# Maxima of the attention pairs half a pair further ahead, two PSUM banks for them and four for the scores, and 97-row weights loaded as 96 + 1 rows

## The reference, cut to what matters

```
qkv = win @ qkv_w.T + qkv_b                      # 192 inputs and a bias row: 97 rows for the second half
attn = einsum('bnd,bmd->bnm', q * scale, k)      # + rel_h + rel_w, both made from q
attn = softmax(attn, axis=-1)                    # 196 positions of a window
out = (attn @ v) @ proj_w.T + proj_b
```

## Time and profile before

| what | value |
|---|---|
| median of 3 runs (lowest, highest) | 718.72 us (714.18, 724.86) |
| the profiled execution's own time | 724.53 us |
| its span, first to last instruction | 722.6 us |
| busy: TensorE, VectorE, ScalarE, POOL | 85%, 41%, 30%, 19% |
| mean granted TensorE clock | 0.864 |
| images turned and projected | from 14 to 81 us |
| position terms, maxima of pair 0 | 81 to 125.5 us |
| pairs 0 to 5 start at | 125.5, 153.9, 181.1, 205.1, 233.9, 261.3 us |
| granted clock rises to 1.00 in pairs 0 to 4 at about | 139.7, 170.4, 190.9, 221.6, 249.0 us (steps 3 to 5) |
| and falls to 0.50 at about | 153.4, 187.5, 204.6, 235.3, 262.6 us |
| last product of pair 5 ends | 290.9 us |
| DMA moved | 53.6 MB |

### The profile page before, as it was taken

One profiled execution on the slowest core, in us unless ns is written; L12 is line 12 of the kernel. 1 busy time (PEld: TensorE's weight loads), 2 busy tenths in 40 slices (PEclk: granted clock), 3 DMA queues, 4 the chain that ended last, 5 costly groups with the idle time before them and its releaser, 6 DMA issues.

```text
span 722.6 us, 13520 instructions
## 1 busy us (share of the span) xinstructions
PE 612.8 (85%) x4592; PEld 498.3 (69%) x4593; DVE 294.5 (41%) x899; ACT 220.4 (30%) x554; POOL 137.1 (19%) x113
## 2 busy tenths in 40 slices
PE   0599989979978979899999998995079999999991
PEld 0477886746655755855558896785069999999991
DVE  4353444635735521711123363454613333333331
ACT  1013322334333333132232323132024444444440
POOL 7020100610000000000000031404403333333332
PEclk9999955677968675799999997986579999999997
DMA  2722575937527440490000000104313233233321
GB/s 84 168 66 63 178 185 110 189 102 106 76 37 101 71 78 9 138 414 40 1 1 0 1 29 17 44 1 137 89 29 45 44 44 42 43 43 44 44 37 17
DMA packets 32969, 53.63 MB, mean 74 GB/s; under 512 B 6458, under 2 KB 26484, under 8 KB 31410
## 3 DMA queue, kind: packets, MB, share of 16 engines
q1 hardware_dynamic: 24962, 43.51, 25.3%
q0 software_dynamic: 7968, 9.60, 7.8%
HBM read 32.95 MB, written 20.29 MB: 74 GB/s over the span
## 4 chain that ended last, share of the span: by engine, by line
PE 60%; issue 5%; DVE 5%; SPq 4%; DMA 4%; ACT 2%; POOL 2%; DVEq 0%; POOLq 0%
PE ps L1634 10%; PE ps L1620 7%; PE ps L1327 5%; PE ps L1625 5%; PE ps L1465 4%; PE ps L1453 3%; PE ps L1364 3%; PE ps L1318 3%; PE ps L1522 2%; PE ps L1607 2%; POOL xs_d L553 2%; DMA qa<-erow 2%; PE ps L1457 2%; PE ps L1535 1%; PE ps L1553 1%
## 5 line engine op out<-in xcount | busy, mean ns | idle before, releaser
L566 POOL DMA_INDIRECT out<-ys,place_i x39 | 69.2, 1776 | 123.1 <-DMA out<-ys,place_i 101.6
L1634 PE MATMUL ps<-w2e,hts 128*128 x468 | 82.7, 327 | 1.5 <-DVE ys L1164 1.5
L1634 PEld LDWEIGHTS ps<-w2e,hts 128*128 128x128 f32 x468 | 75.1, 190 | 1.9 <-issue 1.8
L872 DVE TENSOR_REDUCE negm<-ps 98x2 f32<-98x392 f32 x96 | 49.1, 554 | 50.8 <-PE ps L1282 50.4
L553 POOL DMA_INDIRECT xs_d<-rows,slot_i x32 | 31.6, 987 | 192.6 <-DVE slot_i L1076 184.1
L742 ACT ACTIVATE hts<-ps,wst 128x128 f32<-128x128 f32 x234 | 64.5, 383 | 2.2 <-PE ps L1625 2.2
L1327 PE MATMUL ps<-qa,ka 48*98 48x196 f32 x384 | 57.4, 431 | 8.4 <-ACT pt L635 6.1
L635 ACT ACTIVATE pt<-ps 98x392 f32<-98x392 f32 x96 | 42.5, 494 | 61.4 <-PE ps L1327 61.4
L1620 PE MATMUL ps<-xst,wst 128*128 128x128 f32 x468 | 60.0, 279 | 1.1 <-ACT xst L575 1.1
L1620 PEld LDWEIGHTS ps<-xst,wst 128*128 128x128 f32 x468 | 58.4, 195 | 1.7 <-issue 1.7
L575 ACT ACTIVATE xst<-ps 128x256 f32<-128x256 f32 x39 | 15.0, 384 | 121.8 <-PE ps L1607 121.8
(11 more groups left out here) (212 smaller groups left out, 1006.0 us busy)
## 6 DMA issues: line engine op xcount, KB each, us to landing
w1e<-in_w1e SPq DMA_DIRECT2D x8, 579.0 KB, 11.2
w2e<-in_w2e SPq DMA_DIRECT2D x8, 576.0 KB, 12.0
xs<-xs_d SPq DMA_DIRECT2D x39, 98.0 KB, 2.0
ka<-k_d SPq DMA_DIRECT2D x12, 170.0 KB
k_d<-kst SPq DMA_DIRECT2D x16, 121.5 KB, 1.9
x<-in_xp SPq DMA_DIRECT2D x4, 384.0 KB, 19.2
q_d<-qt SPq DMA_DIRECT2D x2, 768.0 KB, 5.5
qa<-q_d SPq DMA_DIRECT2D x12, 128.0 KB
```

The lines of the kernel that those rows point to most:

```text
L566: nc.gpsimd.indirect_dma_start(acc, bass.IndirectOffsetOnAxis(ap=place_i[:, j % 2:j % 2 + 1], axis=0), ys[:, j % 2, :], None, compute_op=A ...
L872: nc.vector.tensor_reduce(dst, src, X, ALU.max, negate=True).then_inc(s["m_red"], 1)
L1634: last = mm(ps[:, 5, 0:D], hts[:, u, k, :], w2e[:, ds(e, 1), k, :], start=(k == 0), stop=(k == HT - 1))
```

## The change

- `wqkv`, `wproj` and `wb`, which have 97 rows, are each loaded by two DMAs, of 96 rows and of 1; semaphore counts follow.
- The maxima of a pair are made in two halves. In pair p, steps 0 to 4 hold units 10 to 19 of p+1, two a step, step 5 none, and steps 6 to 9 units 0 to 9 of p+2 (2, 3, 3, 2). The turn of p+1 is at step 6. Units 0 to 9 of pair 1 stand before pair 0, behind `relative(3)`.
- Product 4 of the pair before and the waits for values, f32 loads and maxima rows stand between units 10 and 11 and the scores of step 0.
- Banks: maxima 0 and 1, the turned maxima in 1; scores 2, 3, 4, 7. A maxima unit waits for the reduction two units back; a score step for the exponentials of two steps back.
- SyncE in pair p: stores of p-1, f32 loads of p+1, maxima rows of p+1, then, when the maxima matmuls of p+1 are done, the bf16 loads of p+3. Those of pair 2 stand before the loop, behind a wait for the stores of the position terms. VectorE's and SyncE's loops over pairs are written out.

The core of the diff (the waits for 13 in place of 11 loads are left out on VectorE and TensorE):

```diff
@@ -55,12 +55,14 @@
-MAX_AT = [range(a, b) for a, b in ((0, 2), (2, 4), (4, 6), (6, 9), (9, 13), (13, 17), (17, 20))] + [range(0)] * 3
-MAX_BANKS = (0, 1, 7)
-SCORE_BANKS = (2, 3, 4)
+MAX_AHEAD = 10
+MAX_AT = [range(a, b) for a, b in ((10, 12), (12, 14), (14, 16), (16, 18), (18, 20), (20, 20),
+                                   (0, 2), (2, 5), (5, 8), (8, 10))]
+MAX_BANKS = (0, 1)
+SCORE_BANKS = (2, 3, 4, 7)
 LINKS = 31
 INVERT_AT = 2
-TURN_AT = 7
+TURN_AT = 6
@@ -290,7 +292,8 @@
             sp.dma_start(ident[:], a["ident"]).then_inc(s["ident_in"], 16)
-            sp.dma_start(wqkv[:], a["wqkv"]).then_inc(s["w1_in"], 16)
+            sp.dma_start(wqkv[0:C], a["wqkv"][0:C]).then_inc(s["w1_in"], 16)
+            sp.dma_start(wqkv[C:C + 1], a["wqkv"][C:C + 1]).then_inc(s["w1_in"], 16)
             for j in range(1, 4):
@@ -383,37 +386,39 @@
             load_pair(1, 1, 0)
-            def pair_step(p, n, more, rows=True):
-                if more:
-                    sp.wait_ge(s["m_ps"], 20 * p + 20)
-                    load_pair(p + 2, n, 1)
-                if rows:
-                    max_rows(p + 1, 1 - n)
+            for k in range(2):
+                sp.wait_ge(s[f"rel_out{k}"], 64)
+            load_pair(2, 0, 1)
+            def store_outputs(p, to_dram):
                 sp.wait_ge(s["o_ok"], 1 + 2 * p + 2)
...
                         src = ot[r:r + HD, :, :].rearrange("p k t -> p (k t)").rearrange("p (bp t) -> p bp t", bp=4)
-                        if more:
-                            dst = o_d[ds(HD * e + 2 * HD * p, HD), :]
+                        if to_dram:
+                            dst = o_d[HD * e + 2 * HD * p:HD * e + 2 * HD * p + HD, :]
                         else:
...
                         sp.dma_start(dst[:, :, TOK * par:TOK * par + TOK], src).then_inc(s["o_out"], 16)
-                if more:
-                    load_pair(p + 2, n, 0)
-            with sp.Fori(0, NPAIR // 2 - 1) as it:
-                for n in range(2):
-                    pair_step(2 * it + n, n, True)
+            for p in range(NPAIR - 1):
+                n = p % 2
+                if p > 0:
+                    store_outputs(p - 1, True)
+                    load_pair(p + 1, 1 - n, 0)
+                max_rows(p + 1, 1 - n)
+                if p + 3 < NPAIR:
+                    sp.wait_ge(s["m_ps"], 20 * (p + 1) + 20)
+                    load_pair(p + 3, 1 - n, 1)
...
             sp.dma_start(ao[0:2 * HD, 1, :], o_d[C:C + 2 * HD, :]).then_inc(s["ao_in"], 16)
-            pair_step(NPAIR - 2, 0, False)
+            store_outputs(NPAIR - 2, False)
@@ -523,15 +528,17 @@
-            for dst, name in ((wproj, "wproj"), (win, "win"), (wout, "wout"), (wb, "wb"), (dft, "dft"), (idft, "idft"),
-                              (ab1, "ab1")):
+            for dst, name in ((wproj, "wproj"), (wb, "wb")):
+                nc.gpsimd.dma_start(dst[0:C], a[name][0:C]).then_inc(s["w2_in"], 16)
+                nc.gpsimd.dma_start(dst[C:C + 1], a[name][C:C + 1]).then_inc(s["w2_in"], 16)
+            for dst, name in ((win, "win"), (wout, "wout"), (dft, "dft"), (idft, "idft"), (ab1, "ab1")):
                 nc.gpsimd.dma_start(dst[:], a[name]).then_inc(s["w2_in"], 16)
...
-            pool.wait_ge(s["w2_in"], 16 * 11)
+            pool.wait_ge(s["w2_in"], 16 * 13)
             late_op(nc.gpsimd.tensor_scalar(aw1[:, :, 2, :], aw1[:, :, 1, :], -1.0, None, ALU.mult))
@@ -629,15 +636,15 @@
                     if tu < 4:
-                        dst, src = pte[:, tu % 2, tu // 2, :], ps[:, SCORE_BANKS[tu % 3], 0:NIMG * EDGE]
+                        dst, src = pte[:, tu % 2, tu // 2, :], ps[:, SCORE_BANKS[tu % 4], 0:NIMG * EDGE]
                     else:
-                        dst, src = pt[:, (tu - 4) % 8, :], ps[0:98, SCORE_BANKS[tu % 3], 0:2 * WIN]
+                        dst, src = pt[:, (tu - 4) % 8, :], ps[0:98, SCORE_BANKS[tu % 4], 0:2 * WIN]
                     nc.scalar.activation(dst, src, ACT.Exp).then_inc(s["t_exp"], 1)
...
                 act.wait_ge(s["m_turned"], p + 1)
-                nc.scalar.activation(mrow[:, n, :], ps[0:16, MAX_BANKS[2], 0:WIN], ACT.Copy).then_inc(s["m_row_ok"], 1)
-                nc.scalar.activation(erow[:, n, :], ps[0:8, MAX_BANKS[2], 2 * P:3 * P], ACT.Copy).then_inc(s["m_row_ok"], 1)
+                nc.scalar.activation(mrow[:, n, :], ps[0:16, MAX_BANKS[1], 0:WIN], ACT.Copy).then_inc(s["m_row_ok"], 1)
+                nc.scalar.activation(erow[:, n, :], ps[0:8, MAX_BANKS[1], 2 * P:3 * P], ACT.Copy).then_inc(s["m_row_ok"], 1)
@@ -864,11 +871,11 @@
                     dst = negm[0:98, n, 8 * e + b:8 * e + b + 17:16]
-                    src = ps[0:98, MAX_BANKS[mu % 3], 0:2 * WIN].rearrange("p (q k) -> p q k", q=2)
+                    src = ps[0:98, MAX_BANKS[mu % 2], 0:2 * WIN].rearrange("p (q k) -> p q k", q=2)
                 else:
...
                     dst = nege[:, n, 4 * e + 2 * hb:4 * e + 2 * hb + 2]
-                    src = ps[:, MAX_BANKS[mu % 3], :].rearrange("p (q k) -> p q k", q=2)
+                    src = ps[:, MAX_BANKS[mu % 2], :].rearrange("p (q k) -> p q k", q=2)
                 nc.vector.tensor_reduce(dst, src, X, ALU.max, negate=True).then_inc(s["m_red"], 1)
@@ -894,26 +901,31 @@
-            def pair(p, n, first, last):
-                for mu in range(20):
-                    if INVERT_AT <= mu < INVERT_AT + 4 and not first:
-                        sums_out(p - 1, 1, mu - INVERT_AT)
-                    if not last:
+            def pair(p, n):
+                first = p == 0
+                for mu in range(MAX_AHEAD, 20):
+                    step = mu - MAX_AHEAD - INVERT_AT
+                    if 0 <= step < 4 and not first:
+                        sums_out(p - 1, 1, step)
+                    if p + 1 < NPAIR:
                         maxima(p + 1, 1 - n, mu)
-                for step in range(4):
-                    sums_out(p, 0, step)
+                for mu in range(MAX_AHEAD):
+                    if p + 2 < NPAIR:
+                        maxima(p + 2, n, mu)
+                    step = mu - MAX_AHEAD + 4
+                    if step >= 0:
+                        sums_out(p, 0, step)
...
             relative(3)
-            pair(0, 0, True, False)
-            with dve.Fori(0, NPAIR // 2 - 1) as it:
-                pair(2 * it + 1, 1, False, False)
-                pair(2 * it + 2, 0, False, False)
-            pair(NPAIR - 1, 1, False, True)
+            for mu in range(MAX_AHEAD):
+                maxima(1, 1, mu)
+            for p in range(NPAIR):
+                pair(p, p % 2)
             for step in range(4):
@@ -1222,7 +1234,7 @@
             turn_image(0, 0, first=True)
-            pe.wait_ge(s["w1_in"], 16)
+            pe.wait_ge(s["w1_in"], 32)
             with pe.Fori(0, NIMG // 2 - 1) as it:
@@ -1269,11 +1281,11 @@
             def max_unit(p, n, mu):
-                bank = MAX_BANKS[mu % 3]
-                if mu == 2:
+                bank = MAX_BANKS[mu % 2]
+                if mu == 1:
                     pe.wait_ge(s["m_row_ok"], 2 * p)
-                if mu >= 3:
-                    pe.wait_ge(s["m_red"], 20 * p + mu - 2)
+                if mu >= 2:
+                    pe.wait_ge(s["m_red"], 20 * p + mu - 1)
                 else:
@@ -1299,14 +1311,14 @@
                 for q in range(2):
-                    nc.tensor.transpose(ps[0:16, MAX_BANKS[2], 98 * q:98 * q + 98], negm[0:98, n, 16 * q:16 * q + 16],
+                    nc.tensor.transpose(ps[0:16, MAX_BANKS[1], 98 * q:98 * q + 98], negm[0:98, n, 16 * q:16 * q + 16],
                                         ident[0:98, 0:98])
-                nc.tensor.transpose(ps[0:8, MAX_BANKS[2], 2 * P:3 * P], nege[:, n, :], ident[:]).then_inc(s["m_turned"], 1)
+                nc.tensor.transpose(ps[0:8, MAX_BANKS[1], 2 * P:3 * P], nege[:, n, :], ident[:]).then_inc(s["m_turned"], 1)
...
-                pe.wait_ge(s["t_exp"], 1 + 20 * p + (2 * j - 1 if j else 0))
-                banks = [SCORE_BANKS[(2 * j + e) % 3] for e in range(2)]
+                pe.wait_ge(s["t_exp"], 1 + 20 * p + max(2 * j - 2, 0))
+                banks = [SCORE_BANKS[(2 * j + e) % 4] for e in range(2)]
                 if j == 0:
@@ -1365,31 +1377,31 @@
-            def pair(p, n, itp, first=False, last=False):
-                more = not last
-                pe.wait_ge(s[f"lf{n}"], itp * 128 + 128)
-                pe.wait_ge(s["m_in"], 64 * p + 64)
-                pe.wait_ge(s["v_pair"], 2 * p + 2)
-                if more:
-                    pe.wait_ge(s[f"lb{1 - n}"], (itp + n) * 128 + 128)
+            def pair(p, n):
+                first = p == 0
                 for j in range(10):
-                    if first and j == 1:
-                        rel_done(pe, 3)
-                    if more and j == TURN_AT:
+                    if j == TURN_AT and p + 1 < NPAIR:
                         max_turn(p + 1, 1 - n)
-                    mus = list(MAX_AT[j]) if more else []
```

(26 more changed lines are left out.)

## The result

The changed kernel takes **696.57 us** (median of 4 runs, 692.51 to 698.00) against 721.79 us (714.18 to 733.64, 4 runs) for the kernel before: a ratio of **0.9676 [0.9573, 0.9778]**, 3.2% faster. Ratios leave out executions more than 1.5% above the fastest of their kernel; medians and ranges hold all of them. The forecast was 693, with a range from 673 to 709. The profiled execution took 698.0 us (span 696.1), 26.5 less than the one profiled before; its mean granted clock is 0.874, against 0.864.

A forecast was written before the change was run, and what follows sets the result against it. TensorE was taken as the bound, losing time to the wqkv load, border and exponential waits and a low clock. Terms summed to -25.5 us: 699 for the profiled execution, 693 against the median, range 673 to 709.

The forecast's parts named there:

- wqkv: At the start, loading it as 96 + 1 rows uses all DMA engines and ends TensorE's wait: -10.9 us.
- Prologue: Ahead of pair 0, ten maxima units of pair 1 delay the first scores: +7.2 us, bounds +5.2 and +8.
- Borders: Between pairs, all 14.4 us of TensorE's waits for maxima rows go; late landing of those rows gives back +2.
- Four score banks: In score steps, the 8.4 us of waits for exponentials go; bounds -6 and -8.4.
- Two maxima banks: In pairs 0 to 4, maxima units stall on VectorE's reductions: +10 us, bounds +2 and +15.
- The clock: Pairs 1, 3 and 4 run low for 8 us each, 24 us less at half speed: -12; pair 5 stays low.
- The rule by which this term would be 0: Skill's psum-queue depth-cycling: brief, frequent idles while cycling PSUM banks swing TensorE's clock; sum would end 12 us higher.
- D: At the start, the split does nothing, because x tiles and not wqkv hold it: 704 us; chance 0.05.
- E: In all pairs, two banks tie TensorE to VectorE and thinner maxima never lift the clock: 739 us; chance 0.03.
- B: In the pairs, the clock isn't regained and the -12 becomes 0: 705 us; chance 0.22.
- C: At four borders, waits return as f32 loads and rows land, 2 us each: 705 us at worst; chance 0.12.
- A: Pair 5 keeps the high clock too, 13 us less: 680 us; chance 0.20.

The follow-up runs named there:

- f1: The kernel before with one edit, wqkv loaded as 96 + 1 rows; 709.94 us.
- g3: The changed kernel with three maxima banks for the thirty units ahead of pair 0 only; 691.31 us, ratio 0.9470 to the kernel before.
- f4: The changed kernel without the ten maxima units ahead of pair 0, whose own steps hold all twenty of pair 1; 698.58 us.
- i4: The changed kernel with the bf16 loads of pair p+3 ahead of the maxima rows of p+1 on SyncE; 701.45 us, ratio 0.9668 to the kernel before.
- i1: The changed kernel with three score banks and still two for maxima, bank 7 idle; 714.46 us, ratio 0.9793 to the kernel before.
- g1: The changed kernel itself, unedited, timed again; 696.06 us, ratio 0.9619 to the kernel before.
- g2: The changed kernel with three maxima and three score banks as before the change, timed in more rounds; 685.98 us, ratio 0.9463 to the kernel before.
- f2: The kernel before with wqkv split and two maxima, four score banks, in the old order of steps; 716.61 us, ratio 0.9955.
- old banks: The changed kernel with three banks for maxima and three for scores; 688.25 us, and 685.98 us when run again.

## Why the prediction was right, and where it was off

**wqkv: right, -12.4 for -10.9.** The mechanism is as forecast, and f1 gives -13.6. The 1.5 us more in the profile are matmuls: the work between turning image 1 and turning image 2 takes 7.9 us and not 9.3, because more of it has the shorter duration (two matmuls of 256 columns took 1.06 us at 16.74 and 0.60 at 18.44). The prediction reads the share of 0.06 over the whole 16.61 us; it held from 18 to 20 us and in two other stretches of 2 us only. The Trainium skill (DMA: Bandwidth & Descriptors, section "Why a DMA increments its semaphore by 16 and not by 1") says that a transfer is spread over the largest number of engines, up to 16, that divides the slowest dimension of both of its access patterns. By this it is one for 97 rows and 16 for 96. The trace agrees, with a share of 0.06 in those stretches before and 1.09 after.

**A step that the prediction left out: +2.5.** The 20 maxima of pair 0 stand ahead of the pairs and also lost a bank. In the timeline the stops recur every two units there, 0.19 us each, and the stage takes 15.3 us (93.11 to 108.40) and not 12.8. The working had priced the two banks in pairs 0 to 4 alone. With g3 the whole effect ahead of the pairs is 3.5 us, 1.0 of it in the prologue.

**Prologue: right, +8.0 for +7.2.** From the start of `relative(3)` to the first score are 15.55 us (108.40 to 123.95), where 7.58 stood before. In the profile of f4 the same units cost as much inside pair 0.

**Borders: -11.7 of -14.4, with +2 for the landing: right.** Of 2.7 us left, 2.36 stand at pair 5. Most of it is the earlier turn and the work behind it. The order of the queue, to which the prediction gave half of its working, moved the rows by 2 us, not by 5, and cost one border 0.73 us when it was put back (i4).

**Four score banks: -8.4 in waits, right; but the fourth bank is worth more.** Beside two maxima banks it is worth 13 us by the ratios and 18 by the medians (i1), most of it by the clock.

**Product 4 ahead of scores: +2.1 for +2.5.** Of the 3.1 us waited for in L1376, 1.0 stand at the very last product, as before.

**Two maxima banks: sized too high as stalls, with the wrong cause for a part.** In the pairs they are 4.7 us for reductions and 2.1 for the copy of the turned maxima: the turned maxima now lie in bank 1, and unit 1 of step 6 needs that bank. That wait, up to 0.6 us each, was in no step. Together 6.8 for +10.

**The swap as a whole: the term that was most off.** The sum has -8.4 and +10 for it, +1.6 net. With the new order it cost 10 us by the medians and 11 by the ratios (g1 against g2), of which 3.5 to 4.1 lie ahead of the pairs. The waits inside the pairs were rightly of about the same size on both sides; that the clock would change with them (i1) was in no term. The order, in turn, was worth more than its terms: -14.4 + 2 + 2.5 + 7.2 - 1.5 - 12 is -16.2, and 20 to 24 were measured.

**The clock: -15.8 for -12, by a different path.** The time at 0.50 fell by 31.5 us, half of which is 15.8. Forecast were 8 us low in each of pairs 1, 3 and 4, and pair 5 low throughout. Measured were pair 1 low for 13.2 us and pairs 3 and 4 hardly at all; pair 5 rose after 11.7 us. In g1, the same kernel, it was pair 1 that ran high, and pair 2 and half of pair 3 that ran low, with the same sum; so the size is borne out, and the shares of single pairs are not something that a forecast could hit. One sentence of the prediction fell, that pair 5 keeps the low clock (f1 has it rise with the old order as well), and with it the argument that the clock doesn't rise without maxima. By its own signs the forecast holds on pairs 1 to 4 (0.89 where above 0.8 was asked for, and 0.78 in g1), and half fails on pair 5 (0.71 where it asked for 0.5). The rule by which this term would be 0 was not borne out in its size, since 31.5 us less ran low. The clock did go on swinging, though in pairs 3 and 4 of this execution it stayed up through waits of up to 0.7 us.

The measured terms of the pairs: -11.7 - 8.4 + 6.8 + 2.1 - 15.8 = -27.0, and -26.6 were measured. The ten units that left pair 4 (-1.5) come on top, so some 2 us are not attributed. With -12.4, +2.5 and +8.0 ahead of the pairs and +1.8 behind them it closes. The +1.8 was unforeseen too: the output of the last pair, which SyncE stores in `ao` in two halves, is now late by 1.70 us for the projection. The stores of the first half start 3.1 us before the last product ends (259.38 to 262.44), and before it was 7.0 (283.94 to 290.93). f1 and f2 have the wait too (1.02 and 1.52 us), with the old order, and there too the end of pair 5 ran at the full clock.

**The rivals.** D fell with the DMA share. E fell: pair 3 ran wholly at the full clock and pair 4 nearly so (0.96). B fell too. Of C one border is there, with 2.36 us, out of the four that it named. A happened by half: pair 5 took 20.5 us where 29.7 stood before, and this paid for the stalls ahead of the pairs that the sum had left out. That was luck, and so was the total in part: the swap came out some 9 us dearer than its terms and the order 4 to 8 us better.

**What stays open.** The same kernel settles at mean clocks that differ by 0.03 to 0.04 between executions, and no run shows what decides it. That short waits of two sorts in a step keep the clock low is suggested by i1 alone. How the price of the two maxima banks divides between stalls and clock inside the pairs is not settled by g3. No run separates the loops that are written out or the split of `wproj` and `wb`, which the sum has at 0.

## What to carry to other kernels

Price a bank that changes hands everywhere it is used: here the fourth score bank was worth 13 to 18 us and the third maxima bank, taken for it, 24 to 28, and an order that already took away the long waits was worth more without the swap. Where the engine that sets the time can run at either of two clocks, an edit can cost several times what it adds in waits (i1: 2 us more idle, 13 to 18 us more time), so price it over several executions, and compare profiles of executions that took about the same time. A load of 97 rows ran on one DMA engine here and held up the three issues behind it for 16.61 us; 96 + 1 rows cured it.

## What the runs showed of the hardware that was not expected

- The granted clock stayed at 0.50 for 11.70 us in which TensorE was busy 11.65 (pair 5 of the changed kernel), and all through pair 0, busy 30.36 of 31.40 us. It stayed there too while TensorE was busy 13.20 of 13.20 us (start of pair 1). The f32 scores with 48 rows are three quarters of the matmul time in pair 5 and half of it in pair 0. Being busy did not by itself raise it.
- Two profiled executions of one kernel differ in which pairs run at 0.50 (the changed one: pairs 0, 1 and the start of 5, or the start of 0, most of 2 and half of 3), and can differ in how long (old banks: 39.5 and 70.6 us), which makes 9.4 us in the pairs.
- The clock rose in pair 5 with VectorE and ScalarE waits in it and no maxima (0.98 from 253.6 us in the changed kernel, 1.00 from 266 in f1), and in the profiled execution before it never did.
